# Eight buffers instead of four for the down products of a mixture-of-experts layer, with the ScalarE and GpSimd loops written out longer

## What is computed

```python
def _L0_ffn_ref(x, gate_w, w_gate, w_up, w_down):
    TOP_K = 8
    xt = x.reshape(-1, H)
    router_logits = xt @ gate_w.T
    routing_weights = jax.nn.softmax(router_logits.astype(jnp.float32), axis=-1)
    top_w, top_idx = jax.lax.top_k(routing_weights, TOP_K)
...
    g = jax.nn.silu(jnp.einsum('th,ehi->eti', xt, w_gate))
    u = jnp.einsum('th,ehi->eti', xt, w_up)
    y = jnp.einsum('eti,eih->eth', g * u, w_down)
    out = jnp.einsum('eth,te->th', y, full_w)
...
x = x + _L0_xattn_ref(_layernorm(x, axis=-1), ctx_2048, ...)
x = x + _L0_ffn_ref(_layernorm(x, axis=-1), ...)
```

## Time and profile before

| what | value |
| --- | --- |
| median of three executions | 826.98 us |
| span of the profiled execution | 758.7 us |
| PE (TensorE matmul) busy | 708.8 us, 93% |
| PEld (weight load) busy | 584.4 us, 77% |
| DVE (VectorE) busy | 566.7 us, 75% |
| ACT (ScalarE) busy | 434.8 us, 57% |
| POOL (GpSimd) busy | 380.1 us, 50% |

### The profile page before, as it was taken

One profiled execution on the slowest core, in us unless ns is written; L12 is line 12 of the kernel. 1 busy time (PEld: TensorE's weight loads), 2 busy tenths in 40 slices (PEclk: granted clock), 3 DMA queues, 4 the chain that ended last, 5 costly groups with the idle time before them and its releaser, 6 DMA issues.

```text
span 758.7 us, 24265 instructions
## 1 busy us (share of the span) xinstructions
PE 708.8 (93%) x3682; PEld 584.4 (77%) x3683; DVE 566.7 (75%) x1355; ACT 434.8 (57%) x1047; POOL 380.1 (50%) x297
## 2 busy tenths in 40 slices
PE   7999999988788799999999999999999999999994
PEld 5466555656667688889988999889988889888993
DVE  4578888878655488677877878877887778767882
ACT  1775666662035366556666666666667566656662
POOL 2006777767776434443544544434553455444554
PEclk9999999999799999999999999999999999999997
DMA  8996777587898999999999999999999999999995
GB/s 297 361 335 234 261 269 288 215 289 273 291 299 188 184 211 224 218 202 237 215 225 240 225 211 238 224 251 228 244 236 245 211 229 248 243 210 227 220 155 79
DMA packets 174405, 179.85 MB, mean 237 GB/s; under 512 B 36864, under 2 KB 128768, under 8 KB 174368
## 3 DMA queue, kind: packets, MB, share of 16 engines
q0 software_dynamic: 30976, 73.48, 43.0%
q1 hardware_dynamic: 118240, 67.67, 35.1%
q10 hardware_dynamic: 25152, 38.30, 15.6%
HBM read 92.25 MB, written 87.13 MB: 236 GB/s over the span
## 4 chain that ended last, share of the span: by engine, by line
SPq 38%; PE 23%; issue 18%; DMA 7%; POOL 7%; ACT 4%; DVE 2%; ACTq 1%; DVEq 1%; POOLq 0%
SPq L320 23%; SPq L325 8%; POOL x_sorted L512 6%; SPq L439 5%; PE bank L1532 3%; PE bank L1533 3%; PE bank L1539 3%; DMA x_sorted<-xn_kept,slots 3%; DMA x_all<-x_sorted 2%; PE bank L1325 2%; DMA x_sorted<-prob,last_slots 1%; PE bank L1504 1%; ACT prob L670 1%; PE bank L1505 1%; PE bank L1506 1%
## 5 line engine op out<-in xcount | busy, mean ns | idle before, releaser
L569 POOL DMA_INDIRECT out_dram<-ctx_all,x_all x144 | 243.2, 1689 | 276.7 <-issue 131.5
L1532 PE MATMUL bank<-gu_hi,xT_hi 128*128 x576 | 194.7, 338 | 2.1 <-ACT xT_hi L800 1.2
L1533 PE MATMUL bank<-gu_lo,xT_hi 128*128 x576 | 195.6, 340 | 0.0
L813 ACT ACTIVATE ctx_all<-bank 128x512 f32<-128x512 f32 x144 | 86.0, 597 | 104.9 <-issue 78.9
L512 POOL DMA_INDIRECT x_sorted<-xn_kept,slots x96 | 100.0, 1042 | 86.7 <-issue 82.0
L1539 PE MATMUL bank<-gu_hi,xT_lo 128*128 x576 | 137.9, 361 | 0.0
L1208 DVE STREAM_TRANSPOSE x_all<-x_all 128x512 f32<-128x512 f32 x146 | 103.9, 712 | 26.5 <-DMA x_all<-x_sorted 22.2
L1255 DVE SCALAR_TENSOR_TENSOR probT<-probT,x_all,bank 128x192 f32<-128x192 f32 x144 | 59.5, 413 | 79.3 <-ACT probT L821 70.5
L1532 PEld LDWEIGHTS bank<-gu_hi,xT_hi 128*128 128x128 f32 x576 | 108.5, 188 | 10.7 <-issue 5.0
L1533 PEld LDWEIGHTS bank<-gu_lo,xT_hi 128*128 128x128 f32 x576 | 108.4, 188 | 5.6
L800 ACT ACTIVATE xT_hi<-x_all 128x512 fp32r<-128x512 f32 x146 | 91.7, 628 | 34.7 <-DVE x_all L1208 34.6
(11 more groups left out here) (222 smaller groups left out, 1109.7 us busy)
## 6 DMA issues: line engine op xcount, KB each, us to landing
x_all<-x_sorted SPq DMA_DIRECT2D x578, 64.0 KB
gu_raw<-in_w_gate_up_dram ACTq DMA_DIRECT2D x28, 768.0 KB
down_raw<-in_w_down_dram ACTq DMA_DIRECT2D x28, 512.0 KB
x_sorted<-pad_rows SPq DMA_DIRECT2D x1, 8720.0 KB, 31.3
x_all<-in_x_dram SPq DMA_DIRECT2D x8, 512.0 KB, 4.9
ctx_all<-in_ctx_dram SPq DMA_DIRECT2D x8, 512.0 KB, 6.6
out_dram<-x_all SPq DMA_DIRECT2D x8, 512.0 KB, 5.9
gu_raw<-in_w_gate_up_dram SPq DMA_DIRECT2D x4, 768.0 KB
```

The lines of the kernel that those rows point to most:

```text
L569: pool.indirect_dma_start(out=out, out_offset=bass.IndirectOffsetOnAxis(ap=xw[:, k, E:E + 1].bitcast(I32), axis=0), in_=y_sb[:, i, :], in_ ...
L813: act_e.activation(y_sb[:, i, :], bank[6 + i % 2][:], ACT.Copy).then_inc(S["y_evac"], 1)
L1532: pe.matmul(out_gu, xT_hi[:, s, c * P:(c + 1) * P], gate_up(gu_hi, c), start=(c == 0), stop=False)
L1533: pe.matmul(out_gu, xT_hi[:, s, c * P:(c + 1) * P], gate_up(gu_lo, c), start=False, stop=False)
```

## The change

`y_sb` gets eight slots, `YS` = 8, and there are eight `added` semaphores. So `evac_y` waits for the add of eight tiles earlier, and GpSimd, at the first tile of an expert, waits on eight semaphores instead of four. Since the token numbers of a tile are read by its add, the gate rows get 32 blocks in place of 16. The slot of a tile has to be a constant of the program, so ScalarE's loops get bodies of 8 tiles (with 16 written out ahead: `run_tiles(act_e, turns, ffn, 2)`), and GpSimd's loop one of 32 tiles. The last two products go to a slot that is worked out at run time (`evac_last_y`).

```diff
-    LOADS, BLOCKS = HC + 1, 16
+    LOADS, BLOCKS, YS = HC + 1, 32, 8
...
-        y_sb = ctx_all[:, 0:4, :]
+        y_sb = ctx_all[:, 0:YS, :]
...
-        xw_rows = x_all[:, SLOTS + 2:SLOTS + 4, :].rearrange("p a f -> p (a f)")[:, 0:BLOCKS * (E + 1)]
+        xw_rows = x_all[:, SLOTS + 2:SLOTS + 5, :].rearrange("p a f -> p (a f)")[:, 0:BLOCKS * (E + 1)]
...
-        added = [sem(f"added{i}") for i in range(4)]
+        added = [sem(f"added{i}") for i in range(YS)]
...
-        def run_tiles(eng, step):
+        def run_tiles(eng, turns, step, unrolled=1):
 
-
-            turns = load_turns(eng)
-            for k in range(SLOTS):
-                step(0, k)
-            with eng.Fori(1, LEAST // SLOTS) as eight:
+            for n in range(unrolled):
+                for k in range(SLOTS):
+                    step(n, k)
+            with eng.Fori(unrolled, LEAST // SLOTS) as eight:
                 for k in range(SLOTS):
                     step(eight, k)
             with eng.Fori(LEAST // SLOTS, NT // SLOTS) as eight:
...
-            wait_apart(eng, passed, *((added[i], 16 * turns) for i in range(4)))
+            even, odd = eng.snap((turns + 1) >> 1), eng.snap(turns >> 1)
+            wait_apart(eng, passed, *((added[i], 16 * (even if i < 4 else odd)) for i in range(YS)))
...
-                    wait_apart(pool, "pool_passed", *((added[n], 16 * q + 16 * (n < i)) for n in range(4)))
+                    wait_apart(pool, "pool_passed", *((added[n], adds_before(round_of, k, n)) for n in range(YS)))
...
-                                        in_=y_sb[:, i, :], in_offset=None, compute_op=ALU.add).then_inc(added[i], 16)
+                                        in_=y_sb[:, k % YS, :], in_offset=None, compute_op=ALU.add).then_inc(added[k % YS], 16)
...
-            with pool.Fori(1, NT // BLOCKS) as sixteen:
+            with pool.Fori(1, NT // BLOCKS) as round_of:
...
-                if not tile_is_before(q, k, 2):
-                    evac_y(j - 2, (k - 2) % 4, None if tile_is_before(q, k, 6) else 16 * (q + (k - 6) // 4 + 1))
+                if not is_before(eight, k, 2):
+                    evac_y(j - 2, (k - 2) % YS, None if is_before(eight, k, 2 + YS) else 16 * rounds_before(eight, k))
...
-            run_quarters(act_e, turns, ffn)
+            run_tiles(act_e, turns, ffn, 2)
 
             split_act_hi(4 * last + 3, 1)
-            evac_y(4 * last + 2, 2, 16 * last)
-            evac_y(4 * last + 3, 3, 16 * last)
+            act_e.reg_alu(last_reg, last, 1, ALU.max)
+            act_e.reg_alu(before_reg, last_reg, 1, ALU.subtract)
+            act_e.reg_alu(odd_reg, before_reg, 1, ALU.logical_shift_right)
+            for i in range(2, 4):
+                evac_last_y(i, last)
```

More of the change, by code:

```diff
@@ L289, in run_tiles @@
                         step(eight, k)
-            return turns
         def run_quarters(eng, turns, step):
@@ L456, in load_tile @@
                 load_x_part(sp, rows, i, range(HC))
-                block = k % BLOCKS if type(eight) is int else SLOTS * sp.snap((eight + k // SLOTS) & 1, min_val=0, max_val=1) + k % SLOTS
+                block = k % BLOCKS if type(eight) is int else SLOTS * sp.snap((eight + k // SLOTS) & 3, min_val=0, max_val=3) + k % SLOTS
                 load_xw(sp, rows, i, block)
@@ L559, in _, with adds_before, add_tile @@
             first_reg = pool.alloc_register("first")
-            def add_tile(sixteen, k):
-                j, i, q = BLOCKS * sixteen + k, k % 4, BLOCKS // 4 * sixteen + k // 4
+            def adds_before(round_of, k, n):
+                return 16 * (BLOCKS // YS * round_of + k // YS) + 16 * (n < k % YS)
+            def add_tile(round_of, k):
+                j = BLOCKS * round_of + k
                 pool.reg_load(first_reg, first_tile[0:1, bass.ds(j, 1)])
                 with pool.If(pool.snap(first_reg, min_val=0, max_val=1) > 0):
-                    wait_apart(pool, "pool_passed", *((added[n], 16 * q + 16 * (n < i)) for n in range(4)))
+                    wait_apart(pool, "pool_passed", *((added[n], adds_before(round_of, k, n)) for n in range(YS)))
                 wait_apart(pool, "pool_passed", (S["y_evac"], j + 1))
                 pool.indirect_dma_start(out=out, out_offset=bass.IndirectOffsetOnAxis(ap=xw[:, k, E:E + 1].bitcast(I32), axis=0),
-                                        in_=y_sb[:, i, :], in_offset=None, compute_op=ALU.add).then_inc(added[i], 16)
+                                        in_=y_sb[:, k % YS, :], in_offset=None, compute_op=ALU.add).then_inc(added[k % YS], 16)
             turns = load_turns(pool)
@@ L581, in _ @@
                 add_tile(0, k)
-            with pool.Fori(1, NT // BLOCKS) as sixteen:
+            with pool.Fori(1, NT // BLOCKS) as round_of:
                 for n in range(BLOCKS // 4):
-                    with pool.If(BLOCKS // 4 * sixteen + n < turns):
+                    with pool.If(BLOCKS // 4 * round_of + n < turns):
                         for k in range(4 * n, 4 * n + 4):
-                            add_tile(sixteen, k)
+                            add_tile(round_of, k)
         @block.scalar
@@ L813, in evac_y, with rounds_before, evac_last_y, ffn @@
                 act_e.activation(y_sb[:, i, :], bank[6 + i % 2][:], ACT.Copy).then_inc(S["y_evac"], 1)
-            def ffn(q, k):
-                j = 4 * q + k
+            last_reg, before_reg, odd_reg = (act_e.alloc_register(n) for n in ("last_turn", "turn_before_last", "odd_rounds"))
+            def rounds_before(eight, k):
+                return eight if k >= 2 else eight - 1
+            def evac_last_y(i, last):
+                act_e.wait_ge(S["y_done"], 4 * last + i + 1)
+                wait_apart(act_e, "act_passed", (added[i], 16 * (last >> 1)), (added[4 + i], 16 * act_e.snap(odd_reg, min_val=1, max_val=NT // 8)))
+                at = act_e.snap(4 * (last & 1) + i, min_val=0, max_val=YS - 1)
+                act_e.activation(y_sb[:, bass.ds(at, 1), :].rearrange("p a t -> p (a t)"), bank[6 + i % 2][:], ACT.Copy).then_inc(S["y_evac"], 1)
+            def ffn(eight, k):
+                j = SLOTS * eight + k
                 s, o = k % 2, 1 - k % 2
@@ L822, in ffn @@
                 xT_hi_part(j + 2, s)
-                if not tile_is_before(q, k, 1):
+                if not is_before(eight, k, 1):
                     split_act_hi(j - 1, o)
@@ L1198, in block_of @@
             def block_of(q, i):
-                return 4 * (q % 4) + i if type(q) is int else 4 * dve.snap(q & 3, min_val=0, max_val=3) + i
+                return 4 * (q % 8) + i if type(q) is int else 4 * dve.snap(q & 7, min_val=0, max_val=7) + i
             def transpose_x(q, k):
@@ L1547, in _ @@
             last = load_last_turn(pe)
-            run_tiles(pe, ffn)
+            turns = load_turns(pe)
+            run_tiles(pe, turns, ffn)
             transpose_act(4 * last + 3, 1)
```

## The result

The changed kernel takes 914.48 us in the median of four executions (910.96 to 919.53), the kernel before 826.7 us on the same chip (826.38 to 834.0). The ratio is 1.100, 95% interval 1.0952 to 1.1048: 88 us slower. The forecast was 843 us, with 819 to 862 as its range. Its mechanism is there; its sizes were far too small.

A forecast was written before the change was run, and what follows sets the result against it. TensorE, all but full in the expert stage, was taken as the bound. From 827 us: minus 5 for the slots, plus 10 for loop refetches, plus 11 at the end, gave 843 us, range 819 to 862.

The forecast's parts named there:

- mechanism: ScalarE's and GpSimd's longer loop bodies no longer stay resident and are fetched again each round; chance 0.60, 843 us.
- The signs named for it: 60 to 120 instruction packets, ScalarE idle 2 to 3 us every eighth tile, TensorE gaps, over 10 us before the last split.
- Rival 1: ScalarE's 525-instruction body stays resident, leaving only the gain and shorter end: 821 us (816 to 826), chance 0.30.
- TensorE's 467 instructions: Argument for resident code: TensorE's loop body, 315 + 152 instructions, isn't fetched again; its store may differ, though.
- the cushion: In the expert stage, ScalarE's silu can come about 1.4 us after its earliest start without delaying TensorE.
- the cost of one miss in the loop: At ScalarE's closing branches, a 3 us fetch costs TensorE 0.7 us in the mean; 14 branches, 10 us.
- the upper end: Pessimistic case for ScalarE's fetches: 4.5 us a miss, giving 31 us in the loop and 26 at the end.
- knock-on: After a late silu, 0.5 us more lost in what follows TensorE's delayed transpose in that tile.
- the end: ScalarE's empty rounds before the last split: six jumps, four missing, 12 us less 1.3 won, 11 us lost.
- the gain: Eight slots remove ScalarE's waits for adds, shortening TensorE's tile periods in the expert stage: 5 us.
- GpSimd's misses: Refetches of GpSimd's longer loop body, claimed to be hidden by the slots at no cost.
- the 68.3 us "around the span": Time outside the profiled execution's 758.7 us span, added to give 827.0 us as the starting time.

The follow-up runs named there:

- h2: Kernel before with eight slots and both ScalarE's and GpSimd's tiles written out without loops: 852.74 us against 856.12, ratio 0.996.
- f2: Kernel before with ScalarE's tiles written out without a loop, still four slots: ratio 1.007 to the kernel before.
- f3: Changed kernel (eight slots, GpSimd's body of 569) with ScalarE's tiles written out without a loop: ratio 1.005 to the kernel before.
- e2: Kernel before with only GpSimd's loop lengthened to 32 tiles (441 instructions), four slots: 764.46 us, ratio 1.006.
- f1: The changed kernel, word for word, measured again beside other follow-up kernels: ratio 1.102 to the kernel before.
- g1: Kernel before with 60 never-run instructions at the end of each ScalarE loop body (328 in all): 877.63 us, ratio 1.028.
- h1: Kernel before with ScalarE bodies padded to 328 instructions, plus 45 instructions ahead of the first loop: 1001.35 us, ratio 1.172.
- f4: Kernel before with 110 never-run instructions at the end of each ScalarE loop body (378 in all): ratio 1.272.
- e1: Kernel before with only ScalarE's loop bodies lengthened to eight tiles (529 instructions), four slots: ratio 1.110.

## Why the prediction was wrong

**Right: the mechanism, and the kind of evidence.** The reading of the queues (packets of 128 instructions, none fetched twice) and the doubled body gave the cause. The signs named for it came: 152 packets against 60 to 120 named, 68 of them between 360 and 680 us, ScalarE idle before the silu every eighth tile, TensorE idle before the transposes, over 10 us between the last silu and the last split. Rival 1 is refuted by the packets. Two signs were larger than named: the packets, and ScalarE's idle, 2.9 to 7.1 us instead of 2 to 3. TensorE's 467 instructions were no argument, as the prediction itself had feared: its queue fetched nothing again while ScalarE's did. The rule of the Trainium skill ("Runtime: NRT & Kernel Launch", "Instruction fetch mechanics") had the direction. It gives a capacity of 512 instructions, and a loop can't use all of it here: one of 328 missed where it touched a fourth packet, which leaves less than 385. The two needn't disagree: three packets touched and the one more that each round brings would be four, 512 instructions.

**Right: the cushion.** It was put at 1.4 us. At the closing branch shown, 7.11 us of ScalarE less 5.74 of TensorE is 1.37; over the 14 this difference is 0.8 to 2.4, 1.5 in the mean.

**Wrong, by far the most: the cost of one miss in the loop.** The term was 14 branches at 0.7, 10 us. The stage grew by 74.3 us; the last tile's share of that is 20.85 - 3.36 = 17.5 (the periods between the last two L1522 and the last two L1504). That leaves 56.8 for 14 branches, 4.1 us each net, six times the forecast. The failed step is the price of one miss: "the nearest rows are DMAs from issue to landing", and from them "I take 3 us, with 2 and 4.5 as ends". In the prediction's own terms, from the copy's start to the next instruction, it was 3.5 to 7.7 us, 5.7 in the mean, above even the upper end. With 5.7 its formula gives 14 x 3.4 = 48 us. TensorE's idle before the transposes was 3.6 us in the mean, 50 in all.

The trace shows where the time goes. From the start of the last packet of the wait to the silu it is 2.1 to 2.7 us at all 14; from ScalarE's stop to the start of the first it is 0 to 4.1 us. At the three shortest waits the DMA engines were 54 to 82% busy in the first 2 us, at the others 83 to 115% (overlapping packets count twice). At the end, the last three jumps, with only instruction packets on the queues, took 2.8 to 2.9 us each. So full DMA engines are the likely cause of the difference; no run varied the traffic by itself. The rows that I bounded the price by were of the first stage and its start, not of the stage where the fetch would run. And since 3 us lay at the edge of what the cushion absorbs, nearly every further microsecond counted in full.

**Put at nothing: TensorE's clock.** The prediction has 0.5 us of knock-on for each late silu and no term for the clock. In the profile of the changed kernel the tile behind a branch takes 4.64 us in the mean where the clock was halved (nine times) and 3.62 where it was not (five times), and 0.3 us more is lost in the tile of the wait. That is about 1.3 us for each halving, an estimate from these means: 12 us of the stage. It also explains most of the distance of the two profiles, 604.4 and 613.2: in the second TensorE was idle at the branches for 5 us more, and the clock was halved at twelve branches instead of nine, about 4 us. The two tiles at each branch took 73 us more than 3.5 each; that the stage grew by less is because the tiles between lost 16 us less than in the kernel before, the slots' gain and other waits together.

**Wrong in size: the end.** 11 us were forecast, 12 less 1.3; it was 17.5. All six jumps missed, where I took four, and each took 3.2 in the mean, where I took 3. So the price was right here and the count was that of the upper end.

**Wrong in size: the gain.** 5 us were forecast. The two runs without a loop on ScalarE put it at 1.8 us of stage, below what their ratios can tell (h2 against f2: 0.5). The count of waits was right (8 and 12.4 us in the run with four slots), but the step from ScalarE's waits to TensorE's periods took a mean of 0.4 for each, from the one example of 0.6 at 553 us. In the kernel before all tiles but the last lose 29.7 us over 3.5 each, and in f3 25.7: most of that excess never hung on the slots.

**Wrong in size, and small: GpSimd's misses.** They were put at nothing; e2 and the step from f3 to h2 have 4 to 7 us for them.

**Wrong, and without effect on the ratio: the 68.3 us "around the span".** Span and time of an execution lie 2 us apart. The profile and the times of before came from executions that differ in the first stage, and I did not ask why a span should be 68 us short of its time.

**Sum.** In f1 83 of the 85 us are in the stage, and 2 behind it (11.2 us from the last down product to the end of the span, 9.1 before). In the first profile 74 of the 88 are in the stage and 2 behind it. The other 12 would lie ahead of it; the kernel before has no profile on that chip, so this stays open.

## What to carry to other kernels

Before a loop's body is written out longer, count its instructions between head and closing branch, those of waits, register moves and skipped code too, and look where it lies: on ScalarE here a loop is free while it touches three packets of 128 instructions, and costs 4 to 9 us a round as soon as it touches a fourth, even if the added code never runs. Where a packet begins isn't visible in the program, but by this count a loop of up to 256 instructions can't touch four, wherever it lies, and one of 384 or more always does. Between the two a change anywhere ahead of the loop can tip it. The page tells it in one line: packets on the instruction queue beyond what the program fills once. Where a body has to be longer, straight code without a loop cost nothing in the stage here. A critical engine that pauses may also come back at half its clock, so read the granted clock behind each new pause. And a wait that the critical engine's cushion absorbs is worth far less than it lasts.

## What the runs showed of the hardware

- A loop of 328 instructions on ScalarE stays or is fetched again by its place alone: no instruction packet in 300 us, some 20 rounds (g1), and 77 packets in 300 us, some 15 rounds, after a shift by 45 instructions (h1).
- A round that misses brings every packet that it touches and one more: 5 a round for a loop of four packets (h1, f4), 6 for the 529 instructions of e1, five packets. Once one jump leaves the store, nothing of the loop is kept.
- Each jump out of the store waited 2.8 to 4.0 us at the end, where the DMA engines run empty, and 2.9 to 7.1 us at the closing branches among full ones, mostly for two packets of 8 KB.
- A pause of TensorE can cost twice: behind nine of 14 pauses of 0.6 to 5.7 us its granted clock was at 0.50 for 3.4 or 6.8 us.
- The same kernel took 760, 827 to 830 and 855 to 856 us on the chips. The first stage makes the difference: it ends at 220, 290 to 298 and 309 to 312 us. From 60 us to that end the granted clock is 0.97 (before), 0.79 (the changed kernel) and 0.78 (h2) and the transfers run at 273, 193 and 183 GB/s; which of these is cause and which effect is open.
